# Graph network on one Trainium2 core: SiLU over four banks at once, roots on ScalarE, biases on TensorE, and a new hand-written order

## What is computed

```python
# layer 0: filters over all 64 x 64 pairs of a graph, summed over neighbours
x = x + gnn0(relu(layernorm(x)), adj)
# layer 1: hyperbolic attention
h = proj(mobius_matvec(W, h)); h = proj(mobius_add(h, proj(expmap0(b_lin))))
x_loc = logmap(h_i, h_j)                        # for each pair i, j
a = silu(concat(x_self, x_loc) @ att_w1.T + att_b1)
att = sigmoid(a @ att_w2.T + att_b2)
s = sum_j(att * x_loc * mask)
s = silu(concat(x_self, s) @ mlp_w1.T + mlp_b1) @ mlp_w2.T + mlp_b2 + x_self
out = proj(expmap(s, h)); x = x + proj(expmap0(silu(logmap0(out))))
# layer 2: x = x + (D^-1/2 adj D^-1/2 relu(ln(x))) @ W + b
# layer 3: messages = where(deg > 0, adj.T @ (h @ Ws) / deg + h @ Wr, 0)
#          x = x + concat(h, messages) @ W_upd
```

## Time and profile before

| | |
|---|---|
| runs, median (lowest to highest) | 2804.75 us (2801.88 to 2804.91) |
| profiled execution, its own time | 2805.9 us |
| its span, first to last instruction | 2804.1 us |
| PE, DVE, ACT, POOL busy | 85%, 78%, 74%, 71% |
| mean granted TensorE clock | 0.938 of full speed |
| first attention SiLU, last one's end | 1570.7 us, 2683.4 us |

### The profile page before, as it was taken

One profiled execution on the slowest core, in us unless ns is written; L12 is line 12 of the kernel. 1 busy time (PEld: TensorE's weight loads), 2 busy tenths in 40 slices (PEclk: granted clock), 3 DMA queues, 4 the chain that ended last, 5 costly groups with the idle time before them and its releaser, 6 DMA issues. The chain is left out here.

```text
span 2804.1 us, 62869 instructions
## 1 busy us (share of the span) xinstructions
PE 2381.2 (85%) x25104; PEld 1165.4 (42%) x25104; DVE 2179.0 (78%) x3321; ACT 2062.4 (74%) x1932; POOL 1977.2 (71%) x1789
## 2 busy tenths in 40 slices
PE   4899999999999999999972577888888888878754
PEld 2333333333333333333332344455555455545433
DVE  6699898989989899898977456687877787784355
ACT  5888888888888888888852566767677777676631
POOL 0798898889889889888963446576666676665431
PEclk9999999999999999999985798999999999999976
DMA  8799899989989899898811566556565656565510
GB/s 230 173 201 200 194 200 196 202 193 201 201 195 199 196 200 199 196 200 196 197 45 46 87 116 111 114 106 111 115 117 111 113 116 113 105 115 98 80 46 19
DMA packets 312067, 410.25 MB, mean 146 GB/s; under 512 B 91488, under 2 KB 284640, under 8 KB 286688
## 3 DMA queue, kind: packets, MB, share of 16 engines
q1 hardware_dynamic: 311776, 406.23, 69.3%
HBM read 368.38 MB, written 35.65 MB: 144 GB/s over the span
## 5 line engine op out<-in xcount | busy, mean ns | idle before, releaser
L682 POOL TENSOR_TENSOR f_gate<-rfT,f_sq 128x1024 f32<-128x1024 f32 x512 | 1219.0, 2381 | 226.5 <-DVE f_prod L697 150.0
L615 PE MATMUL PS<-f_h,w_W2T 64*64 64x512 f32 x8192 | 998.9, 591 | 10.0 <-PE PS L615 1.8
L697 DVE SCALAR_TENSOR_TENSOR f_prod<-PS,b2l,f_gate 128x1024 f32<-128x1024 f32 x512 | 657.2, 1284 | 147.3 <-PE PS L615 111.4
L1175 ACT ACTIVATE a_silu<-PS,c_att_b 128x1024 f32<-128x1024 f32 x512 | 545.9, 1111 | 263.0 <-PE PS L1019 262.0
L577 ACT ACTIVATE f_h<-PS,c_b 128x1024 f32<-128x1024 f32 x512 | 556.4, 1112 | 167.2 <-PE PS L597 166.4
L689 DVE TENSOR_REDUCE yT<-f_prod 128x16 f32<-128x1024 f32 x512 | 618.5, 1208 | 0.0
L1019 PE MATMUL PS<-a_outer,a_rows 32*128 32x128 f32 x8192 | 415.1, 306 | 197.5 <-ACT a_silu L1175 135.7
L615 PEld LDWEIGHTS PS<-f_h,w_W2T 64*64 64x64 f32 x8192 | 341.3, 133 | 561.2 <-issue 437.2
L597 PE MATMUL PS<-f_gauss,W1two 64*64 64x512 f32 x4096 | 546.2, 595 | 7.1 <-ACT f_gauss L564 4.8
L1019 PEld LDWEIGHTS PS<-a_outer,a_rows 32*128 32x128 f32 x8192 | 335.6, 203 | 428.1 <-issue 182.2
L1339 POOL TENSOR_TENSOR a_outer<-a_by_i,a_by_j 128x256 f32<-128x256 f32 x512 | 345.2, 702 | 184.7 <-PE PS L1019 171.9
(11 more groups left out here) (254 smaller groups left out, 2217.7 us busy)
## 6 DMA issues: line engine op xcount, KB each, us to landing
f_gauss<-in_adj SPq DMA_DIRECT2D x128, 1024.0 KB, 11.6
f_sq<-adj_sq SPq DMA_DIRECT2D x256, 512.0 KB, 8.4
a_rows<-hw_d SPq DMA_DIRECT2D x1024, 64.0 KB
hw_d<-b_xc SPq DMA_DIRECT2D x16, 512.0 KB, 5.0
hw_d<-b_sq SPq DMA_DIRECT2D x16, 512.0 KB, 6.4
b_x<-in_x SPq DMA_DIRECT2D x8, 512.0 KB, 5.2
x_d<-b_x SPq DMA_DIRECT2D x8, 512.0 KB, 9.2
h_d<-b_h SPq DMA_DIRECT2D x8, 512.0 KB, 3.6
```

The source lines that it names most:

```text
L615: PE.matmul(post("message", c)[rows[b], n, :], W2T[rows[k], rows[fh]], hidden(c, n)[rows[k], b, :], start=not second, stop=bool(second)).t ...
L682: GP.tensor_tensor(by_pair(GATE[c % GATE_BUFS][:]), rf, by_pair(squares), ALU.mult).then_inc(s_gate, 1)
L697: V.scalar_tensor_tensor(PR[c % PR_BUFS][:], post("message", c).rearrange("p b n -> p (b n)"), b2l[:, c % 2:c % 2 + 1], GATE[c % GATE_BUFS ...
L1175: A.activation(SI[p % SI_BUFS][:], PS[:, first:first + 2, :].rearrange("p b n -> p (b n)"), ACT.Silu, bias=cols["att_b1"][:]).then_inc(s_s ...
```

## The change

1. One SiLU for all four banks of a set: 128 x 2048 instead of two of 128 x 1024. PE waits for the whole of it before it fills the banks anew, and gives one signal per set. The SiLU output has two buffers of twice the size instead of four.
2. The five roots of each group that POOL made are now sqrt operations on ACT, with the reciprocals and the lower clamp on DVE.
3. The biases bd2 and mlp_b2 are added by PE: ahead of each product a matmul of one row of ones with the bias row, into the same bank. The product of each row with the mapped bias becomes eight matmuls with one column (`whb`, made once from W and the bias) in a fill d of its own, copied out by DVE.
4. The first x load is issued at the end of the filter stage, and the row loads of tile 0 are issued in the pair chain ahead of its stores instead of at the first tick of slot 0.
5. All due times are new; the chains' fills, which had 12 different ones, have 21.

```diff
-SI_BUFS, OUTER_BUFS, OUTER_AHEAD = 4, 4, 2
+SI_BUFS, OUTER_BUFS, OUTER_AHEAD = 2, 4, 2
...
-    "lead": (("y0", 35), ("y1", 35), ("t0", 45.5), ("t1", 46.9375), ("m0", 46.9375), ("m1", 46.9375)),
-    "pair": (("h0", 23.5625), ("h1", 23.5625), ("g", 23.5625), ("y", 23.5625), ("r0", 23.5625),
-             ("r1", 23.5625), ("r2", 23.5625), ("r3", 25.9375)),
-    "mix": (("u0", 13.1875), ("u1", 13.1875), ("v0", 27.5625), ("v1", 27.5625), ("s0", 27.5625),
-             ("s1", 27.5625), ("a0", 27.5625), ("a1", 27.5625), ("z0", 28.0625), ("z1", 28.0625)),
-    "last": (("l0", 15.25), ("l1", 15.25), ("k0", 15.25), ("k1", 17.8125), ("t0", 51.1875), ("t1", 51.1875),
-             ("p0", 57.1875), ("p1", 57.1875), ("p2", 57.1875), ("p3", 57.1875), ("q0", 57.1875),
-             ("q1", 57.1875), ("e0", 57.1875), ("e1", 57.1875)),
+    "lead": (("y0", 19.375), ("y1", 20), ("t0", 27.6875), ("t1", 27.6875), ("m0", 31.9375), ("m1", 44.4375),
+             ("d", 49.375)),
+    "pair": (("h0", 4.75), ("h1", 4.75), ("g", 7.5625), ("y", 7.5625), ("r0", 9.25), ("r1", 9.25),
+             ("r2", 9.25), ("r3", 13.75)),
+    "mix": (("u0", 10.5625), ("u1", 10.5625), ("v0", 15.4375), ("v1", 16.625), ("s0", 16.625),
+             ("s1", 20.375), ("a0", 20.375), ("a1", 20.375), ("z0", 22.25), ("z1", 22.25)),
+    "last": (("l0", 10.9375), ("l1", 10.9375), ("k0", 10.9375), ("k1", 10.9375), ("t0", 28.25), ("t1", 35.5),
+             ("p0", 35.5), ("p1", 35.5), ("p2", 40.0625), ("p3", 40.0625), ("q0", 40.0625), ("q1", 46.375),
+             ("e0", 46.375), ("e1", 51.0625)),
...
+        SP.dma_start(bX[:], x_in[:, 0:GT, :]).then_inc(d_x, 16)
...
-            if g == 0:
-                yield -47.625
-                SP.dma_start(bX[:], d["x_in"][:, nodes, :]).then_inc(d_x, 16)
-            yield 56.75
...
+            if g == 0:
+                yield 31.4375
+                load_rows(0)
+            yield 44.5
             SP.wait_ge(b["vt"], g + 1)
...
-                        if j == 0 and u == 0 and c % 2 == 0:
-                            before(PE, s_silu, 2 * s + c // 2 - 1)
+                        if j == 0 and u == 0 and c == 0:
+                            before(PE, s_silu, s)
                         first = (2 * j + u) * P
                         last = PE.matmul(PS[:, c, first:first + P], ROWS[n][rows_of(c), 2 * k + u, j, :],
                                          OUTER[s % OUTER_BUFS][rows_of(c), j, u * A_BLOCK:(u + 1) * A_BLOCK, :]
                                          .rearrange("p a m -> p (a m)"), start=True, stop=True)
-                        if j and u and c % 2:
-                            last.then_inc(s_pair, 1)
+            last.then_inc(s_pair, 1)
...
-            PE.wait_ge(s_silu, 2 * s + 2)
+            PE.wait_ge(s_silu, s + 1)
...
+        def per_tile_and_bias(n, lhs, rhs, bias, h):
+            free(n)
+            for k in range(HALF_GT):
+                PE.matmul(bank(n)[:, k, :], ones[0:1, :], bias[0:1, :], start=True, stop=False)
+                last = PE.matmul(bank(n)[:, k, :], lhs(h * HALF_GT + k), rhs, start=False, stop=True)
+            last.then_inc(s_fill, 1)
...
-                per_tile(num[f"y{h}"], lambda k: nodes[:, k % HALF_GT, :], lambda k: W["Wd2T"][:], h)
+                per_tile_and_bias(num[f"y{h}"], lambda k: nodes[:, k % HALF_GT, :], W["Wd2T"][:], rows["bd2"], h)
...
+            yield at["d"]
+            if g == 0:
+                PE.wait_ge(s_hb, 3)
+            free(num["d"])
+            for k in range(GT):
+                last = PE.matmul(line(num["d"])[:, k:k + 1], bHT[:, k, :], whb[:], start=True, stop=True)
+            last.then_inc(s_fill, 1)
...
-                per_tile(num[f"z{h}"], lambda k: fST[:, k, :], lambda k: W["Wm2T"][:], h)
+                per_tile_and_bias(num[f"z{h}"], lambda k: fST[:, k, :], W["Wm2T"][:], rows["mlp_b2"], h)
...
-        def silu(p):
-            A.wait_ge(s_pair, p + 1)
-            before(A, s_dot, (p - SI_BUFS) // 2 + 1)
-            first = p % 2 * 2
-            A.activation(SI[p % SI_BUFS][:], PS[:, first:first + 2, :].rearrange("p b n -> p (b n)"), ACT.Silu,
+        def silu(s):
+            A.wait_ge(s_pair, s + 1)
+            before(A, s_dot, s - SI_BUFS + 1)
+            A.activation(SI[s % SI_BUFS][:], PS[:, 0:4, :].rearrange("p b n -> p (b n)"), ACT.Silu,
                          bias=cols["att_b1"][:]).then_inc(s_silu, 1)
...
+            yield 49.875
+            A.wait_ge(b["var"], g + 1)
+            A.activation(sB("svar", 3), sB("var", 3), ACT.Sqrt).then_inc(b["sqrt1"], 1)
...
+            yield 58.4375
+            A.wait_ge(b["n2"], g + 1)
+            A.activation(sB("s19"), sB("s18"), ACT.Sqrt).then_inc(b["sqrt2"], 1)
...
-            yield 33.9375
+            yield 32.5
+            A.wait_ge(f["n1"], g + 1)
+            A.activation(sF("sn1"), sF("n1"), ACT.Sqrt).then_inc(f["sqrt1"], 1)
+            yield 34.125
             A.wait_ge(f["targ"], g + 1)
             A.activation(sF("f"), sF("lam"), ACT.Tanh).then_inc(f["tanh"], 1)
-            yield 47.125
+            yield 39.8125
+            A.wait_ge(f["n2"], g + 1)
+            A.activation(sF("sn2"), sF("n2"), ACT.Sqrt).then_inc(f["sqrt2"], 1)
+            yield 40.375
...
-            yield 56.875
-            A.wait_ge(f["sqrt3"], g + 1)
+            yield 49.875
+            A.wait_ge(f["n3"], g + 1)
+            A.activation(sF("sn3"), sF("n3"), ACT.Sqrt).then_inc(f["sqrt3"], 1)
+            yield 57.125
+            A.wait_ge(f["clamp"], g + 1)
             A.activation(sF("sc"), sF("sn3"), ACT.Tanh).then_inc(f["tanh3"], 1)
 
...
             for h in range(2):
-                yield (15.5, -47.5)[h]
+                yield (9.8125, -37.625)[h]
                 evacuate(num[f"l{h}"], half(gU, h))
...
-            if attends:
-                silu(slot * TICKS + tick)
+            if attends and tick % 2 == 0:
+                silu(slot * SLOT_SETS + tick // 2)
...
-        def root(own, x, inverse, half_x, sq, norms, done, g):
...
-        def at_least(own, x):
...
-            yield 2
-            GP.wait_ge(d_x, (g + 1) * 16)
-            GP.tensor_tensor(bX[:], bX[:], row(rows["bd2"]), ALU.add).then_inc(b["bias"], 1)
-            yield 61.1875
-            for h in range(2):
-                taken(GP, num[f"m{h}"])
-            GP.wait_ge(b["sum1"], g + 1)
-            GP.tensor_tensor(bSQ[:], bMX[:], row(rows["hb"]), ALU.mult).then_inc(b["mhb"], 1)
-            yield -51.25
-            GP.wait_ge(b["var"], g + 1)
-            at_least(own_l, sB("var", 3))
-            root(own_l, sB("var", 3), sB("rstd", 3), sB("h1", 3), sB("w1", 3), sB("svar", 3), b["sqrt1"], g)
-            yield 80.0625
-            GP.wait_ge(b["n2"], g + 1)
-            root(own_l, sB("s18"), sB("s19"), sB("h1"), sB("w1"), None, b["sqrt2"], g)
-            yield -36.125
+            yield 65.125
...
-                yield (40.3125, -56.375)[h]
-                V.wait_ge(b["bias"], g + 1)
+                yield (14, -33.5625)[h]
+                V.wait_ge(d_x, (g + 1) * 16)
...
-            yield 62.4375
-            V.wait_ge(b["mhb"], g + 1)
-            rsum(sB("d4"), bSQ[:])
-            yield 50.1875
+            yield 26.1875
+            filled(V, num["d"])
+            own_l.before(V)
+            V.tensor_copy(sB("d4"), line(num["d"])[:, 0:GT]).then_inc(*takes(num["d"]))
+            yield 10.125
             V.wait_ge(b["sqrt1"], g + 1)
+            recip(sB("rstd"), sB("svar"))
...
+            tt(bSQ[:, 0, :], W["WT"][:], rows["hb"][:], MU)
+            rsum(whb[:], bSQ[:, 0, :], gives=(s_hb, 2))
```

More of the change, by code:

```diff
@@ L779, in fill_numbers, with flow_stage @@
     return numbers
-def flow_stage(nc, own, PS, d, W, WrlT, W3, rows, cols, ident, ones, same, by_a, by_m, w2sel, yT, norm):
+def flow_stage(nc, own, PS, d, W, WrlT, W3, rows, cols, ident, ones, same, by_a, by_m, w2sel, yT, norm, bX, d_x):
     V, A, PE, GP, SP = nc.vector, nc.scalar, nc.tensor, nc.gpsimd, nc.sync
@@ L796, in flow_stage @@
     OUTER = [sb(f"a_outer{n}", [P, 2, BLOCK, BLOCK]) for n in range(OUTER_BUFS)]
-    SI = [sb(f"a_silu{n}", [P, CHUNK]) for n in range(SI_BUFS)]
+    SI = [sb(f"a_silu{n}", [P, 2 * CHUNK]) for n in range(SI_BUFS)]
     ATT = [sb(f"a_att{n}", [P, BANK]) for n in range(2)]
@@ L903, in load_rows @@
             n, g, tl = tile % 2, tile // GT, tile % GT
-            before(SP, s_pair, (tile - 1) * 8)
+            before(SP, s_pair, (tile - 1) * 4)
             if tl == 0:
@@ L999, in attention @@
             tile = slot * GT + tick // 8 + 1
-            if tick % 8 == 1 and 0 <= tile < TILES and tile <= (slot + 1) * GT:
+            if tick % 8 == 1 and 0 < tile < TILES and tile <= (slot + 1) * GT:
                 load_rows(tile)
@@ L1091, in pair @@
                 for r in (slice(0, NODES), slice(NODES, P)):
-                    last = PE.matmul(line(num["y"])[r, k * NODES:(k + 1) * NODES], ones[:], bMX[:, k, r],
```

(5 more changed lines are left out.)

321 lines of the change are left out of this document (148 added, 173 removed).

## The result

The changed kernel takes 2791.38 us (median of 7 runs, 2786.13 to 2797.69), the kernel before 2803.97 beside it (7 runs). The ratio is 0.9965, 95% interval [0.9954, 0.9977]: faster by some 10 us, where the forecast was 75 us. The profiled execution of the changed kernel took 2797.69 us (span 2795.8), 8 us less than that of before.

The account below looks back on a forecast made before the run. The prediction took a loop between ACT's SiLUs and PE's bank fills to set the pace. Middle -36 + 49 - 76 + 12 = -51, start -15, tail -9: together -75 us, from 2804.75 to 2730 us, 8 in 10 from 2665 to 2798.

Parts of the forecast that it names:

- The handoff stays: Between sets: ACT's idle time goes only from 1.07 to 1.09 us, so the merged SiLU gives -36 us.
- Roots on ACT: Attention sets: five roots a slot need table loads at 28 places, 1.76 us each, +49 us.
- Rival B: At table switches: ACT runs empty and pays as much again as a load, +72 us, about 2802; chance 0.03.
- What stands in the loop otherwise: Attention sets: fills, evacuations and squares that lengthen the loop fall from 239 to 163 us, -76 us.
- +12 for waits: ACT's queue: five more waits a slot for VectorE's rows, one in three costing 1.0 us, over seven slots.
- the bias fill: PE fills with a bias: 1.03 + 0.93 = 1.95 us, the four one-row matmuls charged like full ones.
- hand-walk: One slot of the new order priced: 23 us in each of slots 1 to 6, 163 us in all.
- the u and l gap: Where r0 to r2, u and l precede ACT's next SiLU: 5.7 us added, a gap of about 8.7 us.
- the attention weights: In each slot: the attention weights add 0.6 us to their set, as an allowance.
- rival A: ACT's queue: late VectorE rows stop attention; gain gone or about 2840 us, moderate case 2815; chance 0.12.
- Ends: Last stage outside attention: -15 us before the first SiLU (-26 to -6), -9 us in the tail (-20 to 0).
- rival C: Attention loop: the order gives little, about 2804 or 2767 us; chance of 2765 to 2799 is 0.17.

Follow-up runs that it names:

- e2: Kernel before with only the merge made, one SiLU of 2048 columns for each set: 2817.08 us, ratio 1.0055.
- e1: Changed kernel with two SiLUs of 1024 columns per set again, with four SiLU buffers: 2772.25 us, ratio 0.9903.
- e4: Changed kernel with copies in place of the five square roots on ACT, so that they need no table: 2753.25 us, ratio 0.9831.
- e5: Changed kernel with each bias fill's four narrow bias matmuls first and its four products behind them, instead of alternating: 2727.87 us, ratio 0.9751.
- e6: e3 with the tanh of the attention weights one set earlier, behind the slot's first SiLU: 2709.24 us, ratio 0.9698.
- e3: Changed kernel with each bias added by one matmul of 512 columns instead of four of 128, ahead of the products: 2729.34 us, ratio 0.9749.
- e10: Changed kernel with the rows of tile 0 asked for at their old, later place: 2802.13 us, ratio 1.0009.
- e9: e6 with the pair chain's square root and two logarithms on ACT ahead of the mix's evacuations s1, a0, a1: 2730.55 us, ratio 0.9759.
- e11: e9 with two SiLUs and a skewed order of PE's inputs in 12 of 32 sets of a slot, one SiLU elsewhere: 2747.22 us, ratio 0.9821.
- e12: e11 with l0 and l1 evacuated on ACT one SiLU later and the k fills on PE behind the next inputs: 2771.29 us, ratio 0.99.

## Why the prediction was wrong

Two steps failed: one in its mechanism, and one in the size of a term.

**The first is "The handoff stays".** It said that PE's first matmuls could start under the second SiLU before, "but the rest waited for its end", and took 1.09 us for the handoff. The handoff is 1.37. What it left out is the other end of the fill: before, ACT could start on the first half of the banks 0.15 us ahead of PE's last input, and PE left its wait for the SiLU 0.09 us sooner. One operation on four banks takes both away. Of the forecast's -36 us, the shorter SiLU was right (1.967 us for 1.96) and the gap ate it twice: by itself the part is +15 (e2), which is 51 of the 65 us by which the forecast missed. (e1 takes it out of the changed kernel and wins 17, but only 8 of them in the sets that it is about.) The trace of before had the rows for it, which the prediction didn't read; PE's timeline between two free sets there:

```profile
2101.68 0.49 PE L1019 MATMUL PS<-a_outer,a_rows 32*128 32x128 f32 x4 [0.31 <-ACT a_silu L1175]
2102.59 1.16 PE L1019 MATMUL PS<-a_outer,a_rows 32*128 32x128 f32 x28 [0.42 <-ACT a_silu L1175]
```

The 28 records behind the second SiLU take 1.16 us where ACT idles 1.07: a gap shorter than the work in it says that ACT doesn't wait for all of the work.

**Roots on ACT: +49, measured +38 (e4).** The mechanism and the 28 places were right. The price is 4.80 less a free set, and since free sets take 3.34 rather than 3.05, a switch costs 1.46 instead of 1.76; PE's inputs lie under the loads. The dearer rule of the Trainium skill (ScalarE: Activation LUTs, What ACT_TABLE_LOAD costs), a drain on top of the load, isn't seen here either: 1.97 + 1.28 + 0.21 + 1.28 = 4.74 of the 4.80 us are records. Rival B is out.

**What stands in the loop otherwise: -76, +12 for waits; here is the second step that failed, the bias fill.** What is left of the +16.5 when the merge (+14 of the middle, e2) and the roots (+37) are taken off is -35, where -64 was forecast. Two sizes were off in it, in opposite directions. The bias fill was charged at 1.95 us, with 0.93 for its four one-row matmuls "charged like full ones"; alternating with the products it takes 3.3, and at places at half clock 5.8. Undone, the alternation and the clock in that gap give 64 us (e5), so by size this is the larger of the two steps. Had it been as charged, the term would have been about -100, so the hand-walk was too dear elsewhere by some 35 us. It was right at the u and l gap (8.2 for 8.7). It was wrong at the attention weights, put at 0.6: their tanh stood a set later than it could, and cost 3.1 a slot (e6). Where else the walk was too dear was not taken apart.

The ACT waits of +12 were not there: no root or logarithm of a middle slot waits a microsecond for VectorE, so rival A is out. The one wait for VectorE that ACT has in the middle, 17.9 us in seven places ahead of the square behind z, comes of PE's slow z fills, and is 3.2 us in e3.

**Ends.** Ahead of the first SiLU -12.6 for -15: 7.4 by the early rows (e10), the other 5 with the shorter chains, which were not tried one by one. The prediction had the outer products as what comes last there. It is ACT:

```profile
1556.63 0.21 ACT L1231 ACTIVATE b_small<-b_small 128x8 f32<-128x8 f32 x1 [4.72 <-DVE b_small L1427]
1556.85 1.28 ACT L1190 ACT_TABLE_LOAD   x1
```

PE had the banks filled at 1557.65 (1555.56 + 2.09), 0.5 us ahead of the SiLU at 1558.15. What rival A feared, a root that waits for VectorE, is seen at this end, 4.72 us once. The tail came out at -12.2 for -9, and no run takes it apart.

**The sum by runs:** +14 (merge) + 37 (roots) - 35 (order, biases and the rest of the middle, by subtraction) - 25 (ends) = -9, against -8 between the profiled executions. Against the forecast: 50 from the handoff, -12 from the roots, 29 from the clumps with the waits, -1 from the ends, which makes 66 of the 67 us between them. The parts were tried one at a time, some in the kernel before and some in the changed one, and they don't simply add: e1 and e5 both win the clock in the same gap.

The time lies in the wide range of 8 in 10 (2665 to 2798), and in what rival C, "the order gives little", had between 2765 and 2799, but by luck and not by its mechanism, since the SiLU did get to 1.96 us. It would have been luck too had the forecast been hit: e5, with the handoff still at 1.37, takes 2728 us, because the handoff (50 us) on one side and the hand-walk and the roots (35 and 12) on the other cancel.

What the change could have given is in e6: the bias as one wide matmul and the tanh a set earlier, 0.9698 for 0.9965.

## What to carry to other kernels

Merging two operations that share a ring of buffers saves one fixed cost and gives up the handing over of the first half: before merging, compare the idle time with the length of the work that is said to fill it. Where undoing a part wins time, look in which sets: of e1's gain more came with the clock in one gap than with the handoff that it was made for. Where two matmul shapes feed one bank, group them by shape; the accumulation group may span the bank. A wait moved out of the longest gap is worth nothing until the trace shows what had been hidden beside it: three re-orderings (e9, e11, e12) each shortened the gap or the sets that they aimed at, and lost more behind them.

## What the hardware showed that was not expected

- A matmul of 128 columns behind another with as many rows starts its passes 0.11 us apart in e5's trace (8 passes take 1.05 us with the last one's 0.27), for one row as for 128. Where one-row and 128-row matmuls alternate, it takes 0.41 us for two passes instead of 0.22 at full clock, 0.72 at half. The weight loads (PEld) show where it is lost; the changed kernel, then e5:

```profile
2038.49 0.29 PEld L1056 LDWEIGHTS PS<-r_mlp_b,ones 1*128 1x128 f32 x2
2038.90 0.30 PEld L1057 LDWEIGHTS PS<-w_Wm2T,f_st 128*128 128x128 f32 x2
```
```profile
1997.38 0.97 PEld L1058 LDWEIGHTS PS<-w_Wd2T,yT 128*128 128x128 f32 x8
1998.26 0.53 PEld L1050 LDWEIGHTS PS<-f_xc,f_h 128*128 128x128 f32 x4
```

In the changed kernel each load starts only with its own matmul (2038.49, 2038.90). In e5 the load of s1 (L1050) starts at 1998.26, 0.11 us ahead of its matmul (1998.37) and beside the last product of y1, which has 128 rows too; the load of the first product (L1058), which follows one-row matmuls, starts at 1997.38 with its matmul. That product adds to a place written from 0.9 us before on (1996.39), so adding onto a fresh result isn't what costs; the change in the number of rows is what both cases have in common. The Trainium skill (TensorE: Matmul & The Clock Gate, The mechanism) says that a weight load overlaps a matmul in flight only when their row groups differ, and names a background weight buffer beside it. Here loads of 128 rows, whose row groups are the same, are the ones that run beside a matmul in flight.

- A wait of PE in the middle of a set's inputs was left sooner than one ahead of them: 0.06 us after the SiLU's end for the 28 matmuls of e1 (2038.54 to 2038.60), 0.15 for the 32 of the changed kernel (2060.97 to 2061.12).
- PE's clock fell to 0.50 where it had just been busy without a pause: y1 and s1 of the changed kernel, at 2025.42, follow PE work without a pause from 2016.6 on; the clock fell in the inputs at 2022.6, which took 1.8 us instead of 1.17, and y1, s1 and the first half of a0 ran at half clock, until about 2033. With 1.3 us less in each bias fill (e3, e5) the same place stayed at full clock. But so it did in slots 2 to 5 of e1, with the same bias fills and no pause of PE from 2006.7 to 2029 in slot 3. What decides it is not settled.
